# Two copies of the transposed probabilities on one engine: a mega-kernel's first attention phase

## The reference

```python
# layer 0: 16 heads of width 8, no projections of q, k, v
y = layernorm(x)
w = softmax(heads(y) @ heads(ctx).T + mask0)
x = x + relu(merge(w @ heads(ctx)) @ wo.T + wo_b)
x = x + top2_of_8_experts(layernorm(x))      # hidden width 512
# layer 1: the same attention with wq, wk, wv, wo, a clip at +-100 and mask1
x = x + attention1(layernorm(x), ctx, mask1)
x = x + quantised_ffn(layernorm(x))
# layer 2: attention, slot feed-forward; layer 3: attention, shared and routed experts
```

## Time and profile before

| | |
|---|---|
| median of three runs | 2242.12 us (2241.88 to 2245.46) |
| profiled execution, own time | 2251.46 us |
| its span | 2249.7 us |
| VectorE busy | 1504.4 us, 67% |
| ScalarE busy | 1293.4 us, 57% |
| GpSimd busy | 631.6 us, 28% |
| TensorE busy, matmuls | 1895.2 us, 84% |
| mean granted TensorE clock | 0.928 of full speed |

### The profile page before, as it was taken

One profiled execution on the slowest core, in us unless ns is written; L12 is line 12 of the kernel. 1 busy time (PEld: TensorE's weight loads), 2 busy tenths in 40 slices (PEclk: granted clock), 3 DMA queues, 4 the chain that ended last, 5 costly groups with the idle time before them and its releaser, 6 DMA issues.

```text
span 2249.7 us, 50232 instructions
## 1 busy us (share of the span) xinstructions
PE 1895.2 (84%) x17702; PEld 1552.6 (69%) x17706; DVE 1504.4 (67%) x3920; ACT 1293.4 (57%) x4431; POOL 631.6 (28%) x626
## 2 busy tenths in 40 slices
PE   3988988888889888658789889999999988988874
PEld 2776877777778776546666667777777766767664
DVE  5988777777777887666666665757657564645342
ACT  1765655555656666536677766667666554544421
POOL 0003021131411220023334343343443423232421
PEclk9998999999999989857789999999999999999987
DMA  7003344353544100310000011223212222223253
GB/s 230 16 29 98 109 124 136 115 164 115 150 144 137 47 20 6 136 31 19 28 6 15 6 61 36 78 67 96 88 51 66 70 83 88 74 85 92 87 157 114
DMA packets 125127, 184.22 MB, mean 82 GB/s; under 512 B 10320, under 2 KB 82064, under 8 KB 124624
## 3 DMA queue, kind: packets, MB, share of 16 engines
q1 hardware_dynamic: 116688, 164.23, 23.9%
q0 software_dynamic: 8192, 16.79, 2.4%
HBM read 145.52 MB, written 35.45 MB: 80 GB/s over the span
## 4 chain that ended last, share of the span: by engine, by line
PE 38%; DVE 7%; issue 5%; ACT 5%; POOL 1%; DMA 1%; SPq 0%; ACTq 0%; DVEq 0%; POOLq 0%
PE ps L1621 6%; PE ps L1873 5%; PE ps L1847 3%; PE ps L1854 3%; PE ps L1643 3%; PE ps L1659 3%; PE ps L1632 2%; PE ps L1828 2%; ACT pb L2019 2%; PE ps L1650 2%; PE ps L1669 2%; PE ps L1677 1%; PE ps L1820 1%; DVE nm L2359 1%; DVE hT L2157 1%
## 5 line engine op out<-in xcount | busy, mean ns | idle before, releaser
L2019 ACT ACTIVATE pb<-ps,nm 128x128 f32<-128x128 f32 x1024 | 363.1, 376 | 211.8 <-DVE nm L2359 211.6
L2060 POOL TENSOR_TENSOR pb<-pb,rcs 128x512 f32<-128x512 f32 x256 | 268.5, 1050 | 703.7 <-DVE rcs L2367 702.8
L968 ACT ACTIVATE pb<-pb,nm 128x128 f32<-128x128 f32 x1024 | 313.0, 392 | 79.2 <-DVE nm L1191 78.9
L2384 DVE COPY pt<-ps 128x512 f32<-128x512 f32 x128 | 88.3, 690 | 227.1 <-PE ps L1873 227.0
L2019 ACT ACTIVATION_READ_ACCUMULATOR pb<-ps,nm 128x1 f32 x1024 | 221.2, 216 | 0.0
L2359 DVE TENSOR_REDUCE nm<-ps 128x8 f32<-128x1024 f32 x128 | 156.0, 1219 | 71.8 <-PE ps L1854 44.2
L1873 PE MATMUL ps<-w,pb 128*128 128x128 f32 x1024 | 171.2, 293 | 22.2 <-ACT pt L2027 11.5
L1621 PE MATMUL ps<-hT,big 128*128 128x128 f32 x960 | 142.9, 296 | 26.3 <-DVE hT L2162 14.8
L1621 PEld LDWEIGHTS ps<-hT,big 128*128 128x128 f32 x960 | 129.4, 208 | 49.1 <-DVE hT L2162 27.2
L1191 DVE TENSOR_REDUCE nm<-pb 128x8 f32<-128x1024 f32 x128 | 156.2, 1220 | 4.4
L855 PE MATMUL ps<-w,pb 128*128 128x128 f32 x1024 | 151.4, 291 | 7.8 <-ACT pb L968 7.1
(11 more groups left out here) (369 smaller groups left out, 4432.7 us busy)
## 6 DMA issues: line engine op xcount, KB each, us to landing
big<-in_we SPq DMA_DIRECT2D x92, 514.0 KB, 3.6
big<-in_we SPq DMA_DIRECT2D x120, 384.0 KB, 3.0
big<-sorted_in SPq DMA_DIRECT2D x8, 960.0 KB, 6.7
sorted_out<-big SPq DMA_DIRECT2D x28, 256.0 KB
sorted_in<-big SPq DMA_DIRECT2D x4, 1472.0 KB, 12.2
sorted_out<-h_all SPq DMA_DIRECT2D x16, 256.0 KB
hidden<-h_all SPq DMA_DIRECT2D x7, 512.0 KB, 2.9
h_all<-hidden SPq DMA_DIRECT2D x7, 512.0 KB, 3.8
```

What stands on the lines that cost most here:

```text
L968: m = a.activation(pb[:, n % 2, k * S:(k + 1) * S], pb[:, n % 2, k * S:(k + 1) * S], ACT.Exp, bias=nm[:, n % 2, k:k + 1])
L2019: m = a.activation(pb[:, n % 2, e * S:(e + 1) * S], ps[:, score_bank(n) + half, k * S:(k + 1) * S], ACT.Exp, bias=nm[:, n % 2, e:e + 1], a ...
L2060: g_.tensor_tensor(p4, p4, r4.unsqueeze(2).to_broadcast([P, 4, S]), ALU.mult).then_inc(n2["p_normed"], 1)
L2384: v.tensor_copy(pt[:, p % 2, 4 * S:8 * S], ps[:, BANK_T, :]).then_inc(n2["p_lo"], 1)
```

## The change

In iterations without expert tiles the second copy, from bank 3 into the second half of `pt`, moves from VectorE (L1198) to ScalarE. It becomes an activation with the Copy function right behind the copy of the first half (L963), ahead of `work(1, n)` and of the exponentials of unit `n`. ScalarE gets the wait for the second count of `transposed` of that unit; it has already waited for `pv`. It counts `p_lo` up in VectorE's place. These are iterations 1 to 33 and 102 to 128, 60 of the 128 in which a copy is made. In iterations 34 to 101 nothing changes.

```diff
@@ ScalarE's loop
                         if p >= 2:
                             a.wait_ge(s["pv"], p - 1)
                         a.activation(pt[:, p % 2, 0:4 * S], ps[:, 2, :], ACT.Copy).then_inc(s["p_hi"], 1)
+                        if not any(tiles_at(place, n) for place in range(3)):
+                            a.wait_ge(s["transposed"], 2 * p + 2)
+                            a.activation(pt[:, p % 2, 4 * S:8 * S], ps[:, 3, :], ACT.Copy).then_inc(s["p_lo"], 1)
                     work(1, n)
@@ VectorE's loop
                     work(1, n)
-                    if 0 <= n - 1 < NUN:
+                    if 0 <= n - 1 < NUN and any(tiles_at(place, n) for place in range(3)):
                         p = n - 1
                         v.wait_ge(s["transposed"], 2 * p + 2)
                         if p >= 2:
```

## The result

The changed kernel takes 2226.85 us (median of 4 runs, 2220.36 to 2230.61) against 2242.39 us before (4 runs): 15.5 us less. The ratio is 0.9925 with a 95% interval of 0.9899 to 0.9951, so it is faster, and by more than the 9.1 us forecast. It lies inside because the range had room for the clock. The profiled execution took 2230.61 us with a span of 2228.8 us at a mean granted clock of 0.934, against 2251.46, 2249.7 and 0.928.

A forecast was written before the change was run, and what follows sets the result against it. VectorE was taken to bound about six units in ten of the two stretches, TensorE's loop the others. Savings of 4.6 and 4.5 us, together 9.1, took the median from 2242.12 to 2233.0 us, range 2225 to 2244.

The forecast's parts named there:

- The bound: Stretches without tiles: VectorE sets about six units in ten, TensorE's loop the others; mask additions 22 to 24 stay 8.3 us.
- The worth of one copy: On VectorE, each removed L1198 saves 0.60 us at most, 36.0 us for all 60.
- ScalarE's side: Each added copy takes 0.49 us, mostly in idle time; at three q copies it is lost, L776 waiting 1.4 not 0.92.
- The sum over the additions: Walk through the mask additions of both stretches: 4.6 plus 4.5, together 9.1 us saved; 52%, own range 2229 to 2239.
- unit 107: Second stretch: 0.98 us given back here and again at 115, as the loop has little left.
- the steps to additions 104, 112 and 120: Second stretch: each step counted as keeping the full 0.60 us, among 13 such places worth 7.8.
- The start of the tiles: End of first stretch: GpSimd's power and scatters set it; L731 starts near 219.5 instead of 224.13, 4.6 us earlier.
- Addition 127: Among the last mask additions of phase one, which should lie 8 to 9 us earlier than before.
- more than the sum, by the clock: Rival: the long low-clock stretch of TensorE, 167.7 to 184.8, goes away; another 4 us, 2229; 12%.
- VectorE throughout: Rival: VectorE bounds everywhere, so every copy gives its 0.60, 36 us in all, 2206; 4%.
- Slower through ScalarE: Rival: late exponentials in 21 units where the copy waited for TensorE; at most 18.9 us lost, 2252; 10%.
- Absorbed: Rival: the loop takes back kept gains, or the tiles' start doesn't move; 2237.6 and up to no change; 22%.

The follow-up runs named there:

- e3_kept: Kernel before, moving only the 21 copies the sum counted as kept; 2328.25 against 2340.47 us, ratio 0.9944.
- e4_rest: Kernel before, moving only the other 39 of the change's 60 copies; 2347.27 against 2340.47 us, ratio 1.0017.
- the control: The kernel before, unchanged, run again as its own kernel; 2246.15 against 2248.12 us, ratio 0.9998.
- e0_after: The change itself run again, against the kernel before; 2232.50 against 2248.12 us, ratio 0.9936.
- the last group: Four kernels against before (2248.12 us), on a chip at the first measurement's speed: the change again, before unchanged, all but seven copies moved, and a version without L853's matmuls.
- e5_before_fill: Kernel before plus matmuls of no use where TensorE idles (iterations 17, 20, 25, 33, ahead of first tile); 2344.69 against 2346.29 us, ratio 0.9995.
- e9_idle0: The change without iterations 19, 27, 102, 105, 110, 113, 118 and without L853's three matmuls per unit; against before 2237.89 to 2248.12 us, ratio 0.9960.
- e8_all: All 128 copies moved, those of the 68 iterations with expert tiles too, against before; 2337.09 against 2346.29 us, ratio 0.9959.
- e5 to e8: Group on one slower chip, before 2346.29 us: before and change with fill matmuls, the change without seven copies, and all 128 copies moved.
- the filled kernels: Kernel before and changed kernel, both with the same matmuls of no use where TensorE idles; 2344.69 and 2341.61 us, ratios to before 0.9995 and 0.9977.
- e7_best: The change without iterations 19, 27, 102, 105, 110, 113, 118, against before; 2333.19 against 2346.29 us, ratio 0.9932.
- e1 to e4: Group on another slower chip, before 2340.47 us: copies of each stretch alone, the 21 copies counted as kept, and the 39 others.
- the halves: Kernel before with only copies 1 to 33 moved, or only 102 to 128; 2333.06 and 2338.07 against 2340.47 us, ratios 0.9969 and 0.9983.

## Why the prediction came out as it did

*The bound.* Right. VectorE set the pace of long units only, and the loop through the exponentials, the transposes and the scores set the others. The pair 22 to 24 at 8.27 to 8.28 us in every kernel that keeps L853 shows it for these two, and e3_kept against e4_rest for the rest as a whole. (L572 serves layer 0 alone, not both layers of the first stretch as I wrote.)

*The worth of one copy, and ScalarE's side.* Right: 0.60 at unit 23 (4.38 to 3.78), 0.48 to 0.50 for the added copy, 0.49 at the q product, where L776's wait rose from 0.92 to 1.41.

*The sum over the additions.* Right in size: 9.1 us forecast, 9.5 +- 2.1 at equal clock. That it came so close is in part luck, since errors of single terms cancelled. I gave back 0.98 at unit 107 and again at 115; the steps there rose by 0.55 (3.35 to 3.90) and 0.29 (3.36 to 3.65), which makes 1.1 us more gain. Against it, the steps to additions 104, 112 and 120 gained some 0.30 each where I kept 0.60 (5.49 to 5.19), and the step to 22 gained 0.35 (6.20 to 5.85), which makes 1.1 us less. Additions 119 to 127 gained 1.15, where the sum had 1.4 (0.60 twice and 0.2).

*The start of the tiles.* The chain was right, and the size too in the pair of traces whose clocks are closer (0.937 and 0.940 over the execution, where the first pair has 0.928 and 0.934). In the first pair L731 moved by 9.6 us (224.13 to 214.52) and in the sum by 4.6. But the control, with no change made, starts it at 220.33, 3.8 us earlier than the trace of before, and from the control to e0_after, in the same group, it moved by 4.7. Addition 127 moved by 7.4 in that pair, where 8 to 9 were forecast.

*The clock.* This is the term that was mis-sized. The prediction held the clock constant, called a change of it "more than the sum, by the clock", gave it 12% and at most 4 us. In the last group the clock's part was 6.7 us, with 0.006 more clock over the whole run. In the first measurement the profiled executions had 0.934 against 0.928, and the 15.5 us leave about as much beyond the sum. That the time still fell into the range is due to its lower end, 2225, which left room for the clock's case; the sum's own range, 2229 to 2239, missed. The direction had a ground that I had written down: router units get shorter, so TensorE's idle time does. e5_before_fill and e9_idle0 show that filling TensorE's idle time raises the clock and emptying it lowers it. That the change raises it by just this route in all the places isn't shown: between additions 35 and 102, where no copy moved, the two traces of the change took 512.8 and 517.7 us and those of the unchanged kernel 520.4 and 514.4, so chance from run to run is as large as the effect in any one stretch. Which stretches carry the 0.006 is open.

*The rivals.* VectorE throughout: refuted, by e3_kept against e4_rest and by e8_all. Slower through ScalarE: no sign of it. Absorbed: on chips without halts no sign of it, 9.5 +- 2.1 at equal clock. On the two with halts the evidence is divided. On that of e5 to e8 the gain is whole at equal clock: 9.2 +- 3.0 us between the filled kernels, and 10.9 +- 2.3 for e7_best. On that of e1 to e4 the halves give 2.0 and 0.5 us and the 21 kept copies 6.9, each less than forecast. Whether halts swallow part of the gain there stays open.

## What to carry to other kernels

Before counting a saving on the busiest engine, take two neighbouring iterations and look for a loop through the other engines that closes over them. Where it is as long as the engine's own work, the saving is zero, however busy the engine is; only the iterations with extra work on it count. And when a change shortens waits of TensorE, expect that the granted clock may move with it and put a price on that: here 6.7 of 16.2 us came with it on one chip, while between the two filled kernels the clock moved the other way. Compare traces only where their clocks are alike. Give fillers ahead of a wait only where the wait is certain.

## What the hardware showed that I had not expected

- A run's time follows its mean granted TensorE clock closely: 1.1 to 1.3 us per 0.001 on the chip of the last group, with runs of one kernel between 0.927 and 0.937.
- Chips differ: the same kernel before took 2242 and 2248 us in two measurements, 2340 and 2346 on two other chips, with halts of TensorE's stream in the trace ("issue", 0.45 us between two matmuls of one line in the rows above) that the faster traces don't show at these places. What halts it is not known.
- Taking out L853's matmuls of no use made the units of the second stretch some 4% shorter (112.1 against 116.3 us) and yet the whole kernel slower than the change. Its mean clock was 0.9255 against 0.9373, and in its trace the clock of the first stretch is 0.86, against 0.95 or 0.96.
